# Experts of a decoder layer on one Trainium2 core: three fp32r products replaced by one plain float32 product, weights kept in SBUF, routing weight multiplied in ahead of the down product

## The reference

```python
scores = sigmoid(x @ router.T)                    # 16 experts
# two of four groups stay, then the four best experts; their scores are normed to sum 2.5
g, u = x @ gate_w[e].T, x @ up_w[e].T             # 256 -> 128, for 16 routed and 2 shared experts
h = silu(g) * u
routed = sum_e combine[t, e] * (h @ down_w[e].T)  # 128 -> 256; combine is 0 for experts not chosen
out = layernorm(x + routed + shared)              # shared: the two shared experts, weight 1
```

## Time and profile before

| | |
|---|---|
| median of 3 runs | 2397.17 us (2395.24 to 2399.33) |
| span of the profiled execution | 2399.3 us |
| highest of the three runs, beside that span | 2399.33 us |
| experts phase in the profile | from some 1736 us to the end |
| PE, DVE, ACT, POOL busy | 80%, 63%, 38%, 12% of the span |

### The profile page before, as it was taken

The page is one execution under the profiler, slowest core; times in us unless marked ns, Lnnn a source line. Parts: engine busy times, 40 slices in busy tenths (PEclk is TensorE's granted clock), DMA queues, the critical chain, the costliest instruction groups (busy, mean ns, idle before and its releaser), DMA issues. The chain is left out here.

```text
span 2399.3 us, 41683 instructions
## 1 busy us (share of the span) xinstructions
PE 1917.5 (80%) x14336; PEld 1274.2 (53%) x14336; DVE 1504.8 (63%) x3145; ACT 901.3 (38%) x1382; POOL 299.4 (12%) x372
## 2 busy tenths in 40 slices
PE   7928666777738824898999999975639999999998
PEld 4626555555525512343434444423328888888887
DVE  7914333333349855686777888815377777777776
ACT  5514333334303300565655666650122232232322
POOL 2100000000014200111111111114344000000000
PEclk9969888888869965899999999997869999999999
DMA  6932222222147732022112122016551000000000
GB/s 178 216 85 78 75 76 72 68 81 77 54 135 213 212 102 84 23 73 65 60 58 79 54 66 69 19 35 192 170 136 43 28 29 28 2 28 28 19 10 9
DMA packets 181108, 187.47 MB, mean 78 GB/s; under 512 B 95952, under 2 KB 152160, under 8 KB 174816
## 3 DMA queue, kind: packets, MB, share of 16 engines
q1 hardware_dynamic: 165488, 171.64, 24.4%
q10 hardware_dynamic: 15472, 13.84, 2.3%
HBM read 114.60 MB, written 70.46 MB: 77 GB/s over the span
## 5 line engine op out<-in xcount | busy, mean ns | idle before, releaser
L1368 DVE TENSOR_REDUCE sa_piece_max<-sa_ps_m 128x1 f32<-128x512 f32 (+4 forms) x1024 | 486.6, 531 | 182.1 <-PE sa_ps_m L1210 121.6
L1325 ACT ACTIVATE sa_prob<-sa_ps_s 128x1024 f32<-128x1024 f32 (+3 forms) x480 | 374.8, 825 | 366.8 <-PE sa_ps_s L1237 214.9
L1205 PE MATMUL sa_ps_m<-sa_k,sa_q 96*128 96x358 bf16 (+7 forms) x1024 | 268.5, 303 | 5.3 <-DVE sa_piece_max L1368 2.2
L1701 DVE SCALAR_TENSOR_TENSOR mo_acc<-mo_ps_o,mo_comb,mo_acc 128x256 f32<-128x256 f32 x512 | 212.3, 477 | 80.9 <-PE mo_ps_o L149 80.9
L536 ACT ACTIVATE la_phi_kT<-la_ps_kT 128x512 f32<-128x512 f32 x128 | 76.5, 597 | 351.6 <-PE la_ps_kT L472 351.6
L1578 ACT ACTIVATE mo_h_hi<-mo_h 128x512 fp32r<-128x512 f32 x144 | 91.0, 632 | 260.0 <-DVE mo_h L1682 260.0
L472 PE MATMUL la_ps_kT<-la_k,la_omega 99*128 99x512 bf16 x128 | 54.2, 423 | 168.1 <-DMA la_v<-s_v 168.1
L1344 POOL TENSOR_SCALAR_AFFINE_SELECT sa_prob<-sa_prob 128x256 f32<-128x256 f32 x256 | 102.9, 408 | 672.7 <-ACT sa_prob L1325 670.2
L1237 PE MATMUL sa_ps_s<-sa_q,sa_k 99*128 99x512 bf16 (+3 forms) x768 | 180.4, 330 | 2.1 <-ACT sa_prob L1325 2.0
L1203 PE MATMUL sa_ps_m<-sa_km,sa_q 96*128 96x154 bf16 x512 | 124.8, 246 | 65.1 <-DMA sa_vm<-mem 47.3
L576 DVE TENSOR_TENSOR la_att<-la_ps_att,la_cap 128x512 f32<-128x512 f32 x128 | 88.6, 692 | 137.5 <-PE la_ps_att L491 137.5
(11 more groups left out here) (189 smaller groups left out, 3885.1 us busy)
## 6 DMA issues: line engine op xcount, KB each, us to landing
s_y<-la_y SPq DMA_DIRECT2D x16, 512.0 KB, 2.7
s_x<-cl_xn SPq DMA_DIRECT2D x16, 512.0 KB, 5.5
s_y<-sa_y SPq DMA_DIRECT2D x16, 512.0 KB, 2.6
mo_w<-experts SPq DMA_DIRECT2D x18, 384.0 KB
s_q_parts<-pj_parts SPq DMA_DIRECT2D x16, 384.0 KB, 4.1
s_k_parts<-pj_parts SPq DMA_DIRECT2D x16, 384.0 KB, 2.6
la_q<-s_q_parts SPq DMA_DIRECT2D x16, 384.0 KB
la_k<-s_k_parts SPq DMA_DIRECT2D x16, 384.0 KB
```

The costliest lines, as they stand in the source:

```text
L1205: last = nc.tensor.matmul(ps_m[:, s, a - lo:hi - lo], qs, k[g][0:STACK, j, a - MEM:hi - MEM], start=lo > 0, stop=True, skip_group_check=True)
L1325: nc.scalar.activation(dst, src, ACT.Exp, scale=HD ** -0.5).then_inc(expd[s], 1)
L1368: nc.vector.tensor_reduce(piece_max[:, j, t, n:n + 1], ps_m[:, s, 0:hi - lo], AX.X, ALU.max).then_inc(piece_done[s], 1)
L1701: last = nc.vector.scalar_tensor_tensor(acc[:, t], ps_o[:, i % 2, t], comb[:, half, t, i - 1:i], acc[:, t], ALU.mult, ALU.add)
```

## The change

- All products of the experts are plain float32 matmuls: `three_passes` isn't used in this phase, and the parts w_hi, w_lo, x_hi, x_lo, h_hi and h_lo are gone with the instructions that made them. A step has 4 matmuls of 512 columns and 4 of 256.
- The weights of all 18 experts have a place of their own in SBUF, outside the phase (class `Weights`), and SP issues their loads during the last batch of softmax_attention.
- The routing weight is multiplied into silu by DVE (new, line 1702 of the changed kernel), then h = scaled silu x ps_u. The operand cb holds the routing weights of a tile spread over all 128 partitions: [128, 16, 512] float32, 4 MB. To make it, PE transposes the weights of 8 blocks, ACT copies them, SP stores them to DRAM in 8 pieces and loads them back with every row sent to 128 partitions, in 4 DMAs of 4 experts (1 MB) for each tile.
- All 18 experts of a tile accumulate in ps_o; `add_up` is gone, and `sum_up` adds x once for each tile (two instructions).
- DVE's first two `multiply` (the shared experts, which need no routing weight) come before the routing; the routing is done for the first 8 blocks alone, and for the other 24 in pieces of 4 instructions behind each later `multiply`.
- The loops over batches are written out; the output rows have a buffer of their own (xo).

```diff
@@ softmax_attention, SP @@
+                    if last:
+                        weights.load(sp, io, g * ALL_EXPERTS // QUADS, (g + 1) * ALL_EXPERTS // QUADS)
@@ new @@
+class Weights:
+    def __init__(self, nc, ph):
+        self.w = ph.sb("w", [P, ALL_EXPERTS, EXPERT_W])
+        self.w_in = ph.sems("w_in", ALL_EXPERTS)
+    def load(self, eng, io, first, end):
+        for e in range(first, end):
+            eng.dma_start(self.w[:, e], io["experts"][:, e]).then_inc(self.w_in[e], 16)
@@ experts, SP @@
+            def load_cb(n):
+                i, first = n // 2, n % 2 * TB
+                for part in range(CB_PARTS):
+                    rows = io["combT"][part * CB_EACH:(part + 1) * CB_EACH, i, first:first + TB].rearrange("e n t -> e (n t)")
+                    sp.dma_start(cb[:, n % 2, part * CB_EACH:(part + 1) * CB_EACH],
+                                 rows.unsqueeze(0).broadcast_to([P, CB_EACH, TILE])).then_inc(cb_in[n % 2][part], 16)
...
+            sp.wait_ge(turned_sb, 1)
+            store_comb(0, 1)
+            sp.wait_ge(comb_out, 16 * FIRST_BLOCKS)
+            load_cb(0)
+            load_cb(1)
+            for n in range(NT):
...
+                if n >= 1 and n + 1 < NT:
+                    sp.wait_ge(scaled, n * EXPERTS)
+                    load_cb(n + 1)
@@ experts, PE @@
                 for first, ps, ready in ((0, ps_g, g_ps), (UP, ps_u, u_ps)):
                     for a in range(CT):
-                        cols = slice(first + a * INNER, first + (a + 1) * INNER)
-                        last = three_passes(nc, ps[:, s], (w_hi[:, e, cols], w_lo[:, e, cols]), (x_hi[:, half, a], x_lo[:, half, a]),
-                                            start=a == 0, stop=a == CT - 1)
+                        last = nc.tensor.matmul(ps[:, s], w[:, e, first + a * INNER:first + (a + 1) * INNER], xT[:, n % 2, a],
+                                                start=a == 0, stop=a == CT - 1)
                     last.then_inc(ready, 1)
...
+            def project_down(k):
+                n, e = divmod(k, ALL_EXPERTS)
+                pe.wait_ge(multiplied, k + 1)
+                if e == 0 and n >= 2:
+                    pe.wait_ge(summed, n - 1)
                 for t in range(TB):
+                    last = nc.tensor.matmul(ps_o[:, n % 2, t], h[:, k % H_SLOTS, t * P:(t + 1) * P], w[:, e, DOWN:EXPERT_W],
+                                            start=e == 0 and t % 2 == 0, stop=e == ALL_EXPERTS - 1, skip_group_check=True)
                 last.then_inc(o_ps, 1)
...
+            gate_up(0)
+            gate_up(1)
+            for k in range(STEPS):
+                if k == SHARED:
+                    turn_first()
+                if k + 2 == TURN2_AT:
+                    turn_rest(k + 2)
+                if k + 2 < STEPS:
+                    gate_up(k + 2)
+                project_down(k)
@@ experts, DVE @@
+            def multiply(k):
+                n, e = divmod(k, ALL_EXPERTS)
+                dve.wait_ge(silu_done, k + 1)
+                if e >= SHARED:
+                    part, first = divmod(e - SHARED, CB_EACH)
+                    if first == 0:
+                        dve.wait_ge(cb_in[n % 2][part], 16 * (n // 2 + 1))
+                    tt(scaled_silu[:, k % 2], silu[:, k % 2], cb[:, n % 2, e - SHARED], ALU.mult).then_inc(scaled, 1)
+                    dve.wait_ge(scaled, routed_before(k) + 1)
+                dve.wait_ge(u_ps, k + 1)
+                if k >= H_SLOTS:
+                    dve.wait_ge(o_ps, k - H_SLOTS + 1)
+                source = silu if e < SHARED else scaled_silu
+                tt(h[:, k % H_SLOTS], source[:, k % 2], ps_u[:, k % 2], ALU.mult).then_inc(multiplied, 1)
...
+            multiply(0)
+            multiply(1)
+            for _ in route(0, FIRST_BLOCKS):
+                pass
+            rest = route(FIRST_BLOCKS, ALLB)
+            for k in range(2, STEPS):
+                multiply(k)
+                for _ in range(ROUTE_OPS):
+                    next(rest, None)
```

More of the change, by code:

```diff
@@ L1507, in _ @@
[L1507 to L1511 removed]
+            load_xT(0)
+            sp.dma_start(ident[:, :], io["ident"]).then_inc(ident_in, 16)
+            load_xT(1)
+            for n in range(2):
+                load_x(n)
+            sp.wait_ge(turned_sb, 1)
+            store_comb(0, 1)
+            sp.wait_ge(comb_out, 16 * FIRST_BLOCKS)
@@ L1528, in gate_up @@
                     last.then_inc(ready, 1)
-            def project_down(b, half, es, i):
-                n, s = tile(b, half), i % 2
-                pe.wait_ge(h_split, n * ALL_EXPERTS + es[-1] + 1 + START)
-                pe.wait_ge(added, n * SUMS + max(0, i - 1) + START)
-                for t in range(TB):
-                    for e in es:
-                        tokens = slice(t * P, (t + 1) * P)
-                        last = three_passes(nc, ps_o[:, s, t], (h_hi[:, e % H_SLOTS, tokens], h_lo[:, e % H_SLOTS, tokens]),
-                                            (w_hi[:, e, DOWN:EXPERT_W], w_lo[:, e, DOWN:EXPERT_W]),
-                                            start=e == es[0], stop=e == es[-1])
-                last.then_inc(o_ps, 1)
@@ L1568, in _, with copy_comb @@
-            for e in range(HI_ON_ACT):
-                act.wait_ge(w_in[e % W_SLOTS], 16 * (e // W_SLOTS + 1) + START)
-                nc.scalar.activation(w_hi[:, e], w[:, e % W_SLOTS], ACT.Copy).then_inc(w_hi_done, 1)
-            with act.Fori(0, B) as b:
-                for half in range(HALVES):
-                    for e in range(ALL_EXPERTS):
-                        count = tile(b, half) * ALL_EXPERTS + e + 1 + START
-                        act.wait_ge(g_ps, count)
-                        nc.scalar.activation(silu[:, e % 2], ps_g[:, e % 2], ACT.Silu).then_inc(silu_done, 1)
-                        act.wait_ge(multiplied, count)
-                        nc.scalar.activation(h_hi[:, e % H_SLOTS], h[:, e % 2], ACT.Copy).then_inc(h_hi_done, 1)
+            def copy_comb(i, first, end, src):
+                act.wait_ge(turned, i)
+                nc.scalar.activation(combT[:, first:end].rearrange("p n t -> p (n t)"), src, ACT.Copy).then_inc(turned_sb, 1)
@@ L1580, in _ @@
+            for k in range(STEPS):
+                if k == SHARED + 2:
+                    copy_comb(1, 0, 1, ps_o[:, 1, 0, 0:P])
+                if k == TURN2_AT:
+                    copy_comb(2, 1, ALLB // FIRST_BLOCKS, ps_g[:, k % 2, 0:ALLB // FIRST_BLOCKS * P - P])
+                act.wait_ge(g_ps, k + 1)
+                nc.scalar.activation(silu[:, k % 2], ps_g[:, k % 2], ACT.Silu).then_inc(silu_done, 1)
         @blk.gpsimd
@@ new lines, in sum_up, with first_stats @@
+            def sum_up(n):
+                dve.wait_ge(o_ps, (n + 1) * ALL_EXPERTS)
+                dve.wait_ge(x_in[n], 16)
+                for t in range(0, TB, 2):
+                    last = tt(z[:, t:t + 2], ps_o[:, n % 2, t:t + 2], x[:, n % 2, t:t + 2], ALU.add)
+                last.then_inc(summed, 1)
+            def first_stats(n):
+                dve.wait_ge(summed, n + 1)
+                for t in range(TB):
+                    last = nc.vector.bn_stats(stats[:, t], z[:, t])
+                link(last)
@@ L1741 @@
+            sum_up(NT - 1)
+            first_stats(NT - 1)
+            last_stats(NT - 1)
+            normalise(NT - 1)
 SCRATCH = {
```

416 lines of the change are left out of this document (190 added, 226 removed).

## The result

| | before | after |
|---|---|---|
| median in the same series | 2396.2 us (2395.1 to 2399.3, 4 runs) | 2522.9 us (2520.9 to 2527.2, 4 runs) |
| after / before | | 1.052, 95% interval 1.050 to 1.054 |
| span of the profiled execution | 2399.3 us | 2519.7 us |
| end of the phase before, to the end | 664.4 us (from 1734.88) | 788.0 us (from 1731.66) |

A forecast was written before the change was run, and what follows sets the result against it. TensorE's own work was taken to bound the experts stream. Stream +141.1 us, start -17.7 and tail +0.2 sum to +123.6, giving 2521 us, slower by 5.1%; range 2504 to 2555 us, held at 0.86.

The forecast's parts named there:

- step of the stream: Experts phase, gate and up of one expert, down of another: 5.16 us for 4.18, over 144 steps +141.1 us.
- to the first product: Start of experts: PE's first product comes 13.0 us after the phase before ends (1734.9 to 1747.9), 5.3 us earlier.
- clock at the first product: Start of experts: PE begins at the lower clock and loses 1.84 us, as before the change.
- idle ahead of gate_up 4: Start of experts: PE idle 16.4 us until routing weights pass through DRAM and DVE makes its first scaled products.
- clock after it: Start of experts: PE's clock falls again with the idle stretch, another 1.84 us.
- other engines' work gone: Experts stream: work taken off ACT, DVE and POOL ends no wait of PE, so it is worth nothing there.
- cb against the stream: Experts stream: each 4.2 MB cb tile loads within 93 us of stream, 45 GB/s, against 250 to 340 seen.
- tail: After the last matmul: keeps its 10.4 us; `sum_up` 0.3 us shorter, one more barrier, together +0.2 us.
- A pass is a pass: Rival, experts stream: each of a plain product's four passes costs an fp32r pass; 59.6 us more, 2581 us; chance 0.08.
- The first weights come late: Rival, start of experts: cb's 8 DMAs served side by side, first 1 MB after 33 us, 2550 us; chance 0.07.
- cb can't keep up: Rival, experts stream: cb loads bind below 45 GB/s; at 40 a tile takes 105 us, 2605 us; chance 0.04.
- Faster than before: Rival, experts stream: 512-column records at 0.229 us, a step 2.78 us, some 2179 us in all; chance 0.02.

The follow-up runs named there:

- e3: Changed kernel with the 18 weight loads moved from softmax's last batch to the start of the experts phase: 2527.5 us, ratio 1.052.
- e2: Changed kernel with three fp32r products of the high parts in place of each plain product, operands rounded by ACT, POOL and DVE: 2391.7 us, ratio 0.995.
- e7: Changed kernel with cb traffic of tiles 2 to 7 doubled by one spare 1 MB DMA ahead of each real one: 2523.0 us, ratio 1.050.
- e8: Changed kernel with three spare 1 MB DMAs ahead of each real cb load in tiles 2 to 7: 2584.4 us, ratio 1.076.
- e1: Kernel before with each three fp32r products in experts replaced by one plain float32 product of the high parts: 2538.4 us, ratio 1.056.
- e4: Changed kernel with cb of the first two tiles loaded at the phase's start from another DRAM tensor (w1), so wrong routing weights: 2512.6 us, ratio 1.046.
- e6: Changed kernel with cb loaded in 16 DMAs of one expert (256 KB) instead of 4 of four experts (1 MB): 2523.7 us, ratio 1.051.
- e9: Kernel before, 8 blocks routed first, POOL's splits paused meanwhile, ACT rounding 3 weights, fourth weight loaded before SP's routing wait: 2378.3 us, ratio 0.991.
- e10: Kernel before with 8 blocks routed first, ACT rounding 3 weights, fourth loaded before SP's routing wait, POOL's splits not paused: 2383.0 us, ratio 0.993.

## Why the prediction was right, step by step

| term | predicted | measured | from |
|---|---|---|---|
| step of the stream | 5.16 us, 743.0 for 144 | 5.16, some 743.6 | 1743.1 to 2509.3, less the waits, the cold clock and the transposes below |
| to the first product | 13.0 | 11.4 | PE's timeline |
| clock at the first product | 1.84 | 1.9 | ps_g and ps_u take 3.57 and 1.80 us from start to start, in place of 1.72 each |
| idle ahead of gate_up 4 | 16.4 | 16.2 + 0.9 | PE's timeline |
| clock after it | 1.84 | 2.35 | 3.54 and 2.25 us in place of 1.72 each, at a granted clock of 0.50 in the first |
| transposes of the other 24 blocks | 1.3 | 1.2 | the step with them takes 6.34 us (1897.37 to 1903.71) in place of 5.16 |
| weights loaded in softmax | 0 | 0 | e3 |
| other engines' work gone | 0 in the stream | 0 | e2: 4.18 us with DVE at 37% |
| cb against the stream | hidden at 45 GB/s | hidden, at 90 too; not at 181 | e7, e8 |
| tail | +0.2 | 0.0 | 10.4 us from the last matmul to the end |
| sum, experts phase | +123.6 | +123.6 | 788.0 - 664.4 |

**The stream.** The argument rested on reading one operation in another phase, and on the choice of that row over the router's product. The stream of after and e1 both show 0.43 us a record of 512 columns. The router's 0.46 us a record, which the prediction took as the upper bound and as support for the rival of four fp32r passes, was a misreading of the earlier trace rows. The four records last 1.90 us from the first start to the last end, against 1.88 for four of 128 stationary columns in the stream, and the records themselves are as long (0.59 us): their starts are 0.44 us apart. The remaining 0.1 us of the 1.84 lies between the last of them and the next kind of instruction. So that row spoke for 0.43 as well. *A pass is a pass* is ruled out: a quarter of a plain product is 0.214 us at 512 columns, and an fp32r pass 0.229 in the same phase, also in e2, where the rest of the kernel was that of after.

The rule of the Trainium skill that the prediction weighed (FP8 and Floating Point Precision, TensorE Precision Notes), four passes for true FP32, would have given 59.6 us too much when read as a price of 4/3. Whether it is right as a count, no run here shows: they have the time of a product, not its passes.

**The start.** The net of it was right to 0.4 us (34.4 us predicted; 11.4 + 1.9 + 17.1 + 2.35 + 1.2 make 34.0), but that is partly luck: inside it two terms were mis-sized and offset each other. The way of the small stores through DRAM took about 1.4 us from the last issue to the first load, not 3.5: I had scaled it from one of 256 KB. The first 1 MB of cb took 9.7 us from issue to use, not 6.4: I had priced it at the 250 GB/s of plain loads, and these loads ran at 162, while the same loads from another tensor ran at 383 (e4). The routing (10.35 us for 10.2), the transpose and copy (0.8 for 0.7) and the eight stores (3.2 us to the last issue for 3.0) were as priced. The first wait was 1.6 us shorter than priced and the clock behind the stall cost 0.5 more; the kernel before had lost 2.4 us there (twelve matmuls from 1786.03 to 1791.22, 5.19 us in place of 2.75), nearer to it than the 1.84 that I carried over from its first product. That the sum agrees with the phase to the tenth is chance: single executions differ by more, and the medians are 127 us apart. e4 shows that the stall is this way, and that 14.4 us of the phase hang on it, not the 18 that the wait and its clock loss make, since most of the clock loss stays with a wait of 1.9 us in two pieces, and the clock rose later at that kernel's start.

**The rivals.** *The first weights come late* is ruled out by e6, since the wait shrinks with the size of the first load. *cb can't keep up* is ruled out for this kernel by e7 and shown to be real by e8 at four times the traffic. *Faster than before* needed a record below 0.36 us; it was 0.43.

**Where the expected gain of such a change would have been.** The changed kernel takes 244 us of work from DVE, 100 from ACT and 73 from POOL, and e1 and e2 show that nearly all of it was worth nothing: DVE was waiting for PE in the stream. Its one real gain, at the start (15.6 us against e1, 18 by the terms above), is had without the new product and without cb: e9 takes it, and somewhat more, by splitting the routing and by ordering the weights' splits and loads around it.

## What to carry to other kernels

Three fp32r passes and one plain float32 matmul stand for the same product here (how their errors compare wasn't measured), and the plain one is the dearer by a quarter on TensorE (0.858 against 0.688 us at 512 columns): take it only where TensorE waits for the engines that make the split. Before freeing an engine, look in the stream for what ends last; here the only time to be had was a queue of small work ahead of the first consumer, and a queue is shortened most cheaply by doing first the part that the consumer needs. When such a wait goes, look at once for what is late next: here a new wait in SP's queue and ACT's work behind it took 13 of 21 us until ACT's share was cut to the three weights that are there and the fourth was loaded ahead of SP's wait.

## What the runs showed of the hardware that I had not expected

- Loads that send 2 KB rows to 128 partitions each moved 171 to 175 GB/s from the tensor of the routing weights with the DMA engines at their fullest (e8), and 383 GB/s from another tensor, also with the engines full (e4). The busy share of the DMA engines doesn't tell the two apart (1.01 and 1.06); only the GB/s do. The cause is open.
- A small instruction of DVE with two inputs in SBUF takes 1.7 to 1.8 us instead of 0.18 while POOL makes w_lo (e10); this decided whether a pause of POOL pays. The Trainium skill gives a cause (SBUF — State Buffer, Who interferes with whom): the two engines share a pair of ports under an exclusive lock. The rows agree: the three long ones under POOL's three w_lo end at 1749.26, 1751.05 and 1752.83, 1.8 us apart as those are, the last 0.06 us behind the end of POOL's, 1752.77.
- After two pieces of idle time of 0.9 and 1.0 us around one transpose (e4), ps_g took 3.14 us at a granted clock of 0.57 on average; after 16.2 us (after) 3.54 at 0.50; in the stream 1.72 at 1.00. Taking most of a wait away gave back little of what the clock costs.
